# Adding the batch-norm shift on TensorE in fp32 to every part of the output, with 20 of 32 rows squared on ScalarE from the 14th block on

## What is computed

```python
def reference(x, src, dst, edge_attr_32, W_f, b_f, W_s, b_s, gamma, beta):
    # x: 100000 x 64, 25000 edges, edge_attr_32: 25000 x 32, all fp32
    h = maximum(layernorm(x), 0)                       # per node
    z = concatenate([h[src], h[dst], edge_attr_32])    # per edge, 160 wide
    m = sigmoid(z @ W_f + b_f) * softplus(z @ W_s + b_s)
    message = segment_sum(m, src, 100000)              # 100000 x 64
    mean = message.mean(axis=0)
    var = ((message - mean) ** 2).mean(axis=0)
    normed = (message - mean) * rsqrt(var + 1e-5) * gamma + beta
    return x + h + normed
```

## Time and profile before

| what | us |
|---|---|
| median of 3 runs | 1061.29 |
| profiled execution, its own time | 1060.81 |
| its span in the profile | 1059.1 |
| start to the first load of the scan | 845.3 |
| end of PE's last crossing of the scan | 923.7 |
| first part added (end of line 1801) | 928.3 |
| last part added (start of line 1801) | 1053.9 |
| busy in the span: PE, DVE, ACT, POOL | 631.5, 733.2, 540.0, 729.9 |

### The profile page before, as it was taken

One profiled execution on the slowest core, in us unless ns is written; L12 is line 12 of the kernel. 1 busy time (PEld: TensorE's weight loads), 2 busy tenths in 40 slices (PEclk: granted clock), 3 DMA queues, 4 the chain that ended last, 5 costly groups with the idle time before them and its releaser, 6 DMA issues.

```text
span 1059.1 us, 11028 instructions
## 1 busy us (share of the span) xinstructions
PE 631.5 (60%) x2458; PEld 453.8 (43%) x2458; DVE 733.2 (69%) x1547; ACT 540.0 (51%) x1181; POOL 729.9 (69%) x652
## 2 busy tenths in 40 slices
PE   0474665666566666656766666676556689944232
PEld 0252444454444444444544454554445578810000
DVE  3884675757575686766777666776666569699788
ACT  1263654545454665545565464655646564434322
POOL 6777878787877877777878777787878752430700
PEclk9855565555555565556555555655656689955555
DMA  8997534343434334333443333433433399799999
GB/s 320 397 394 275 126 96 106 96 106 94 106 94 106 74 86 87 61 81 61 79 87 61 80 71 70 87 63 79 85 56 59 35 380 420 247 302 426 413 404 377
DMA packets 88183, 176.07 MB, mean 166 GB/s; under 512 B 42575, under 2 KB 49299, under 8 KB 79699
## 3 DMA queue, kind: packets, MB, share of 16 engines
q1 hardware_dynamic: 35851, 115.32, 30.9%
q0 software_dynamic: 42880, 20.09, 15.4%
q10 hardware_dynamic: 9416, 40.29, 9.3%
HBM read 107.12 MB, written 68.53 MB: 166 GB/s over the span
## 4 chain that ended last, share of the span: by engine, by line
POOL 48%; DMA 24%; issue 17%; DVE 6%; PE 3%; ACT 1%; SPq 1%; POOLq 0%; ACTq 0%; DVEq 0%
POOL msgs_dram L607 24%; POOL m_buf L594 24%; DMA m_buf<-msgs_dram 8%; DMA msgs_dram<-y_kept 8%; DMA msgs_dram<-sums,target 6%; PE ps_all L1544 2%; DVE m_buf L1795 2%; DMA out_dram<-m_buf 2%; DVE m_buf L1801 1%; DVE sums L1717 1%; PE ps_all L1539 0%; SPq L499 0%; POOL m_buf L617 0%; DVE target L794 0%; DVE m_buf L763 0%
## 5 line engine op out<-in xcount | busy, mean ns | idle before, releaser
L594 POOL DMA_INDIRECT m_buf<-in_x_dram,m_buf x384 | 366.9, 955 | 118.7 <-issue 109.4
L607 POOL DMA_INDIRECT msgs_dram<-sums,target x184 | 289.7, 1574 | 56.2 <-issue 55.8
L1171 PE MATMUL ps_all<-sums,m_last 128*128 128x64 f32 x920 | 188.5, 394 | 124.8 <-ACT m_last L1033 107.1
L1171 PEld LDWEIGHTS ps_all<-sums,m_last 128*128 128x128 f32 x920 | 181.0, 303 | 136.2 <-issue 112.5
L719 DVE TENSOR_REDUCE m_last<-late 128x24 f32<-128x1536 f32 (+1 forms) x49 | 85.3, 1742 | 87.8 <-ACT late L984 87.8
L1131 PE MATMUL ps_all<-ident,m_buf 128*128 128x128 f32 x192 | 53.0, 431 | 128.6 <-DVE m_buf L809 128.6
L1145 PEld LDWEIGHTS ps_all<-m_buf 128*128 128x128 f32 x392 | 91.9, 322 | 49.0 <-issue 49.0
L794 DVE TENSOR_TENSOR target<-moved,m_last 128x4 int32<-128x4 f32 x49 | 9.6, 196 | 146.1 <-POOLq L605 145.8
L1033 ACT ACTIVATE m_last<-m_last,one_col 128x512 f32<-128x512 f32 x196 | 107.6, 550 | 1.6
L1131 PEld LDWEIGHTS ps_all<-ident,m_buf 128*128 128x128 f32 x192 | 34.9, 217 | 160.4 <-DVE m_buf L809 138.5
L1143 PE MATMUL ps_all<-m_buf 128*128 128x512 f32 x98 | 98.8, 1111 | 0.0
(11 more groups left out here) (171 smaller groups left out, 1078.1 us busy)
## 6 DMA issues: line engine op xcount, KB each, us to landing
m_buf<-msgs_dram SPq DMA_DIRECT2D x38, 1024.0 KB, 11.9
m_buf<-in_x_dram SPq DMA_DIRECT2D x48, 512.0 KB, 5.0
msgs_dram<-y_kept SPq DMA_DIRECT2D x14, 1536.0 KB, 11.0
out_dram<-m_buf ACTq DMA_DIRECT2D x20, 1024.0 KB, 11.2
m_buf<-src_rows_dram SPq DMA_DIRECT2D x47, 256.0 KB, 4.1
y_spill_dram<-y_kept ACTq DMA_DIRECT2D x19, 512.0 KB
y_kept<-y_spill_dram SPq DMA_DIRECT2D x8, 1024.0 KB, 12.1
m_buf<-in_x_dram,m_buf POOLq DMA_INDIRECT x392, 2.5
```

Of the source, the lines that this page charges most:

```text
L594: pool.indirect_dma_start(xg[:, n % G_SLOTS, 2 * j + c, :], None, x, bass.IndirectOffsetOnAxis(ap=ids[:, c, n * TILES + j:n * TILES + j + ...
L607: pool.indirect_dma_start(msgs, bass.IndirectOffsetOnAxis(ap=target[:, n % UNROLL, j:j + 1], axis=0), comb[:, n % COMB_SLOTS, j, :], None, ...
L1171: pe.matmul(ps_c[:, j, :], same_of(b, j, j + 1)[:, 0, :], msg_of(g)[:, b, :], start=(b == 0 and not begun), stop=(b == j), skip_group_chec ...
```

## The change

There are two parts. The scan no longer takes the mean out of six parts, PE no longer adds beta in it, and the split into three bf16 rows is gone. PE adds the shift, in fp32, from the one partition where it lies to all 33 parts, with `ones[0:1, :]` as weights, once `shift_ready` is given; DVE makes the shift before it multiplies part 0. And ACT squares 20 of 32 rows in all blocks from 13 to 23, in three banks from block 15 on.

```diff
-SQ_THEN_ROWS = 16
+SQ_THEN_ROWS = 20
-SQ_CHANGE = 19
+SQ_CHANGE = 15
-BETA_PARTS = Y_FIRST + 2
-FEW_SQUARED = 2
-FEW_ROWS = 12
...
-        if b >= NB - 1 - FEW_SQUARED:
-            return [(0, n, FEW_ROWS)]
...
-        def add_row(k, weights, row):
+        def add_row(k):
...
-                ins = pe.matmul(ps_y(k)[:, c:c + w, :], weights, row.unsqueeze(1).to_broadcast([row.shape[0], w, F]),
+                ins = pe.matmul(ps_y(k)[:, c:c + w, :], ones[0:1, :],
+                                shift[0:1, :].unsqueeze(1).to_broadcast([1, w, F]),
...
-            if Y_BLOCK < b <= Y_BLOCK + Y_FIRST:
-                pe.wait_ge(affine_loaded, 32)
-                add_row(b - Y_BLOCK - 1, ones[0:1, :], bet[0:1, :])
...
-        for k in range(Y_FIRST, BETA_PARTS):
-            add_row(k, ones[0:1, :], bet[0:1, :])
-        pe.wait_ge(split_done, 1)
-        for k in range(BETA_PARTS, len(y_parts)):
-            add_row(k, ones_b[:, :], shift_row[0:SPLIT, :])
+        pe.wait_ge(shift_ready, 1)
+        for k in range(len(y_parts)):
+            add_row(k)
...
-            if order[0] + 2 <= b < order[0] + 2 + BETA_PARTS:
-                take_mean(b - order[0] - 2)
...
-        dve.wait_ge(mean_taken, BETA_PARTS)
+        dve.wait_ge(chain, 3)
+        dve.tensor_tensor(shift[:, :], bet[:, :], mean2[:, :], ALU.subtract).then_inc(shift_ready, 1)
...
-            if k == BETA_PARTS:
-                split_shift()
             m = m_out(i, r, n)
             wait_m(dve, i)
+            if i < len(held):
+                dve.wait_ge(block_crossed, order[i] + 1)
```

## The result

The changed kernel takes 1101.63 us (median of 4 runs, 1101.26 to 1101.85), the kernel before 1061.15. The ratio is 1.0383, 95% interval 1.0365 to 1.0401: 40.5 us slower. The forecast was 1099.5 in a range from 1094 to 1105.

A forecast was written before the change was run, and what follows sets the result against it. Before, PE bound the scan's end and transfers the output; afterwards PE's half-clock matmuls would bind. Shift ready at 925.5 plus 166.9 us gives 1092.4; the ending makes the span 1097.7, own time 1099.4, forecast 1099.5 us, range 1094 to 1105.

The forecast's parts named there:

- The deciding term: Output, fp32 one-row shift matmuls: half clock throughout, 97 at 1.71 us plus one of 1.07, together 166.9 us of PE.
- PE's input would be in time: Output, per 32-row part: DVE's add and ACT's store and copy take 4.6 us, covered by PE's 6.84, 2.2 to spare.
- Rival B: Output: never-resting one-row matmuls get full clock, transfers bind again, 1058 to 1061 us, not slower; chance 0.10.
- the 4 us of the earlier trace: Kernel before, 927.60 to 931.60: one-row matmuls kept PE busy at clock 0.50, taken as evidence for half clock.
- the chance of 0.85: Probability given to the main forecast, half clock throughout the output.
- The start of the stream: Variance to output: shift ready at 925.5 us, and only then can PE start on part 0.
- in block 13 an addition of 0.5 us more: Scan: block 13's extra DVE addition, taken as lost in waits, block 14 still at 896.78; price otherwise 0.5 us.
- The ten blocks and the correction: Scan's end on DVE: ten blocks at 2.10 us are 21.0, then the correction's reduction takes 1.40 to the next start.
- The sums over partitions at half clock: Before the variance: ten small instructions after PE idles, 2.1 us taken in place of 1.41, at most double.
- the signs that I gave for the scan: Scan's profile: crossings end by 916, diagonal starts about 921 behind DVE's reduction, variance at 923 to 925.
- The end: Output's close: 5.2 us from the last addition's start to the span's end, up to 1.5 less with empty DMA queues.
- The terms up: Upper bound: block 13's 0.5 us, variance 0.7 later, handovers up to 0.1 at 33 parts, median 1, 0.5 more; 1105.

## Why the prediction was right

**The deciding term.** 97 matmuls at 1.71 us and one of 1.07 made 166.9 us; measured 166.99. That PE's input would be in time held as well: in the stream of 167 us no gap was left, and DVE waited 48.0 / 20 = 2.4 us before a 32-row addition, where I had said 2.2. The Trainium skill, "TensorE: Matmul & The Clock Gate", "Why this matters for your kernels", asks only for continuous busyness; the traces of 1, 32 and 64 rows differ from that (0.50 for 60 us of 60 busy), those of 96 and 128 agree. Rival B falls as the change was written. With a deeper operand its full clock comes, and its 1058 to 1061 us with it once block 13 is left alone (1060.87).

**How well the rows carried it.** The evidence was thinner than I made it. I took the 4 us of the earlier trace rows, one-row matmuls at 0.50 with PE never idle, as a sign that the clock would not rise, because the crossings had needed less. But the streams of 128 dense rows and of 96 rows also had 5.0 and 5.3 us at half clock, and the crossings behind the bank clearing of the changed kernel some 5 us (901.70 to about 906.8), and then their clock rose. So 4 us at half clock could not tell a stream that stays there from one that does not. That the depth decides was shown only by the runs; the chance of 0.85 owed something to luck.

**The start of the stream** was 3.4 us too early: 925.5 forecast, 928.89 measured. Most of it is block 14, which started 3.07 us later than I took. The step "in block 13 an addition of 0.5 us more", which I had lost in other waits, cost 2.68 us, since I had counted the instruction and not the order on ACT's queue, where its chunk stood behind a copy that waits for PE; 0.39 us lay before it. The ten blocks and the correction from there to the reduction took 923.32 - 899.85 = 23.5 us, against 23.4 in the sum (919.5 + 0.7 - 896.78). The sums over partitions at half clock took from 924.69 to 927.16, 2.5 us for my 2.1: the upper half of the bounds I gave (1.41 to 2.8). So the signs that I gave for the scan did not come: the crossings ended at 919.6 and not by 916, the diagonal started at 924.26 and not about 921, and the variance at 927.16 and not between 923 and 925. Nor was the first reload at 943.65 but at 947.66, which cost nothing here.

**The end** was 1.4 us too late. From the start of the last addition to the end of the span I took 5.2 us of the earlier trace rows; it was 1099.8 - 1095.97 = 3.8; from 1050 to 1095 the DMA share was down to 0.51 (1.5 us of that stood in the lower bound). With 0.1 us more of stream the errors leave 2.1 us between the spans, 1097.7 and 1099.8.

**Slips in the sum.** By its own working, 1099.4 for the profiled execution and 0.5 for the median, the forecast should have read 1099.9, 1.7 us under the 1101.63 and not 2.1. The terms up add to 1105.5, where 1105 was given. And "DMA share well under 1" held for the mean (0.83), not for 960 to 1000 us, where it was 1.01.

**What rival B said of a faster scan** was wrong in one respect. I held that little of an earlier output start would arrive, as the reloads begin at 943.65. In the run with identity and old squares the first reload was issued at 945.84, later than before, and 2.2 of the 4.8 us arrived in the span. This suggests that the start of the additions and stores counts for more than that of the reloads; no run was made to part the two.

**The gain that was there.** Removing beta and the six mean subtractions from the scan did bring the first addition forward by 4.8 us, when squares were left as they were. Moving four more rows to DVE's side gave it away: with identity weights 1057.89 us became 1060.87 with block 13 left alone, and 1065.94 with it. DVE already had 22 of 30 us to do there, and PE, which it was to relieve, had been relieved of its four beta rows by the same change.

## What to carry to other kernels

Before a matmul is put in fp32 because "PE is idle there", price its passes at the clock that the stage will be granted, with operands of the depth that it will have. Where the value to be added lies in all partitions anyhow, an identity as weights costs no more columns and here kept the clock up. And when an instruction is added to one engine, look at what stands before its input in the other engine's queue: here an addition of 0.42 us brought a wait of 2.22.

## What the runs showed of the hardware

- A stream of fp32 matmuls of 512 columns that never rested stayed at half clock for 167 us with operands of 1, 32 and 64 rows (1101.4 to 1101.6 us). With 128 rows the clock rose 3.4 us (identity) and 5.0 us (dense) after the stream's start, with 96 rows after 5.3 us, and was 1.00 and 0.99 from 934 to 994. I had expected 64 rows to suffice.
- The values did not matter to the time: identity and dense weights gave 1065.94 and 1065.80 us.
- Two streams that began at full clock, 3.6 us after the last crossing, lost it: one row after 1.5 us (at 922.6, begun at 921.15), 128 rows after 1.4 us (at 922.9, begun at 921.55). The second had it back at 926.2, the first never.
- In both kernels two small instructions of DVE ended when POOL's additions on 128 x 768 did. In the changed one those on 128 x 4 values took 1.32 and 1.74 us in place of 0.16 and ended within 0.02 us of POOL's (895.05 and 895.04, 896.93 and 896.91); why was not tested.
